# Mixture-of-experts stage: six steps of token rows in flight, the fifth group's weights in the last group's early place, later weights asked for over steps 3 to 12

## The reference

```
x = x + tanh(g_xattn[0]) * mamba(ctx_1024, layernorm(x))
x = x + tanh(g_ffn[0])   * moe(layernorm(x))
x = x + tanh(g_xattn[1]) * cross_attention(layernorm(x), ctx_1024, mask)
x = x + tanh(g_ffn[1])   * bitlinear_ffn(layernorm(x))

# moe: E = 64 experts, K = 8 choices a token, H = 256, I = 96, CAP = 64 places an expert
w, sel = top_k(softmax(x @ gate_w.T), K);  w = w / sum(w)
inp[e, slot] = x[tok]                        # the first 64 tokens that chose expert e
h   = silu(inp @ wg[e]) * (inp @ wu[e])      # (64 x 256) @ (256 x 96), twice
out = h @ wd[e]                              # (64 x 96) @ (96 x 256)
y[tok] += out[e, slot] * w
```

## Time and profile before

| what | value |
|---|---|
| median of 3 runs | 581.57 us (579.41 to 582.18) |
| profiled execution: own time | 579.86 us |
| profiled execution: span of the page | 577.9 us |
| mean granted TensorE clock | 0.953 of full |
| PE busy over the span | 478.6 us (83%) |
| DVE busy | 473.6 us (82%) |
| ACT, POOL busy | 365.2 us (63%), 280.9 us (49%) |
| DMA | 48.63 MB, mean 84 GB/s |

### The profile page before, as it was taken

How to read it: one execution, slowest core, us unless ns; L and a number is a source line. 1 busy time by engine, 2 the same in 40 slices (tenths; PEclk the granted TensorE clock), 3 DMA queues, 4 the chain that set the end, 5 groups by cost and what they waited for, 6 DMA issues and landing times.

```text
span 577.9 us, 10286 instructions
## 1 busy us (share of the span) xinstructions
PE 478.6 (83%) x3070; PEld 361.1 (62%) x3080; DVE 473.6 (82%) x1249; ACT 365.2 (63%) x831; POOL 280.9 (49%) x263
## 2 busy tenths in 40 slices
PE   5817777757769889999899999998789988998735
PEld 3302222122348856776788999997689878997714
DVE  4899999999995737888666856996899969875887
ACT  2785555535434645688776666679656796679543
POOL 4118777869420465550278368623875243323211
PEclk9956999999997989999999999999999999999877
DMA  5939400001052979894412012400335000000000
GB/s 155 233 76 325 120 0 1 1 1 36 1 157 80 308 217 294 212 313 144 180 52 73 2 29 65 56 1 2 47 55 66 0 2 2 19 2 0 1 19 20
DMA packets 45626, 48.63 MB, mean 84 GB/s; under 512 B 5660, under 2 KB 42118, under 8 KB 45574
## 3 DMA queue, kind: packets, MB, share of 16 engines
q1 hardware_dynamic: 41734, 36.46, 22.2%
q0 software_dynamic: 3840, 11.54, 9.3%
HBM read 41.43 MB, written 6.56 MB: 83 GB/s over the span
## 4 chain that ended last, share of the span: by engine, by line
PE 37%; DVE 21%; issue 20%; POOL 9%; ACT 7%; DMA 3%; SPq 1%; DVEq 1%; POOLq 0%; ACTq 0%; another core or an unknown queue 0%
DVE hst L1880 7%; PE ps L1619 6%; PE ps L1558 5%; PE ps L1559 5%; PE ps L1560 5%; PE ps L1608 3%; PE ps L1476 2%; DMA G<-token_rows,idx_x 2%; POOL dbu L586 2%; PE ps L1277 2%; POOL G L672 2%; POOL pn L688 2%; DVE hc L1889 2%; POOL G L650 1%; PE ps L1374 1%
## 5 line engine op out<-in xcount | busy, mean ns | idle before, releaser
L688 POOL TENSOR_TENSOR pn<-pr,pinv 128x512 f32<-128x512 f32 x64 | 67.7, 1060 | 87.3 <-DVE pinv L2289 86.9
L586 POOL TENSOR_TENSOR dbu<-du,brow 128x512 f32<-128x512 f32 x64 | 81.5, 1285 | 41.4 <-DVE du L1873 23.1
L1277 PE MATMUL ps<-hc,ident 128*128 128x512 f32 x128 | 72.7, 657 | 27.5 <-DVE hc L1889 26.0
L1880 DVE TENSOR_TENSOR_SCAN hst<-ps,dbu 128x512 f32<-128x512 f32 x64 | 77.6, 1213 | 0.2 <-POOL dbu L586 0.2
L831 ACT ACTIVATE ps<-dtv,amat 128x510 f32<-128x510 f32 x64 | 44.1, 690 | 49.1 <-DVE hst L1880 48.2
L1019 ACT ACTIVATE pr<-ebuf,smin 128x256 f32<-128x256 f32 x128 | 63.7, 501 | 13.7 <-DVE smin L2280 6.9
L1619 PE MATMUL ps<-pT,cS 128*128 128x256 f32 x256 | 66.5, 382 | 0.0
L1277 PEld LDWEIGHTS ps<-hc,ident 128*128 128x128 f32 x128 | 20.3, 195 | 66.8 <-DVE hc L1889 63.6
L650 POOL DMA_INDIRECT G<-token_rows,idx_x x32 | 38.1, 1192 | 48.3 <-DVE wkv L2015 24.0
L672 POOL DMA_INDIRECT G<-expert_out,idx_g x48 | 51.6, 1074 | 11.6 <-issue 10.2
L2280 DVE CUSTOM_DVE_ANT_0 ebuf<-ps,mbias 128x256 f32<-128x256 f32 x128 | 48.9, 419 | 4.1 <-issue 4.0
(11 more groups left out here) (380 smaller groups left out, 1377.3 us busy)
## 6 DMA issues: line engine op xcount, KB each, us to landing
wdn<-in_L_ffn_wd SPq DMA_DIRECT2D x12, 384.0 KB, 9.6
wgu<-in_L_ffn_wg SPq DMA_DIRECT2D x11, 384.0 KB, 7.0
wgu<-in_L_ffn_wu SPq DMA_DIRECT2D x11, 384.0 KB, 9.7
expert_out<-xn SPq DMA_DIRECT2D x11, 256.0 KB, 6.8
wq<-in_L_xattn_Wq SPq DMA_DIRECT2D x2, 1024.0 KB, 9.2
wo<-in_L_xattn_Wo SPq DMA_DIRECT2D x1, 2048.0 KB, 15.7
wo<-in_L_ffn_w SPq DMA_DIRECT2D x2, 1024.0 KB, 7.0
expert_out<-pexp SPq DMA_DIRECT2D x5, 256.0 KB, 3.3
```

The lines of the kernel that those rows point to most:

```text
L586: nc.gpsimd.tensor_tensor(dbu[:, j, :], du[:, j % 2, 512 * hb:512 * hb + 512], brow[:, j // 2, :], ALU.mult).then_inc(pool_dbu, 1)
L688: nc.gpsimd.tensor_tensor(pn[:, h % 2], pr[:, h % 2], pinv[:, h % 2, :].unsqueeze(2).to_broadcast([P, 2, L]), ALU.mult)\
L1277: pe.matmul(bank(2 + j % 2), ident[:], hc[:, j % 2, :], start=(isinstance(m, int) and m + k == 0), stop=(isinstance(m, int) and m + k == N ...
L1880: V.tensor_tensor_scan(hst[:, j, :], bank(j % 2), dbu[:, j, :], 0.0, ALU.mult, ALU.add)\
```

## The change

The row ring grows from four groups to six (`ROWS = 6`), which takes the place of group 4's gate and up weights in `G`. Two semaphores of a later stage serve the two new places, and that stage's waits are raised by 64 for it. POOL's gathers of groups 4 and 5 wait for `wqT_in_psum`, those from 6 on for `hg_ready` of group g-6. Group 4 takes the early places `wgu_last` and `wdn_last`; group 12 goes to the same places once group 4 is done, and groups 8 to 11 and 13 to 15 go to the ring. SP asks for gate and up of groups 8 to 15 in steps 3, 4, 5, 7, 8, 9, 10 and 11, for down one step later each. On TensorE `gate_up` of groups 1 and 2 is put ahead of `turn_rows` of groups 2 and 3.

```diff
+ROWS = 6
...
+        gate_up_homes = [*(wgu[:, k] for k in range(RING)), wgu_last[:], *(w[:] for w in early_gate_up)]
+        down_homes = [*(wdn[:, k] for k in range(RING)), wdn_last[:], *(w[:] for w in early_down)]
+
+        def home(g):
+
+            if g < 2 * RING:
+                return g
+            return (g - 2 * RING) % (RING + 1)
...
+        xe_flat = G[:].rearrange("p a k h -> p (a k h)")[:, 0:ROWS * 2 * ROW]
+        xe = xe_flat.rearrange("p (s q w) -> p s q w", s=ROWS, q=2)
...
             def gate_up_load(g):
-                slot = gate_up_slot(g)
-                if g == RING:
-                    sp_.wait_ge(wqT_in_psum, NKV)
-                elif RING + EARLY < g < NG - 1:
-                    sp_.wait_ge(gu_done, g - 7 if g < 12 else g - 3)
...
+                if g > RING + EARLY:
+                    sp_.wait_ge(gu_done, g - 7 if g <= 3 * RING else g - 4)
...
             def down_load(g):
-                if g == RING:
-                    sp_.wait_ge(down_done, 1)
-                elif RING + EARLY < g < NG - 1:
-                    sp_.wait_ge(down_done, g - 6 if g < 12 else g - 3)
...
+                if g > RING + EARLY:
+                    sp_.wait_ge(down_done, g - 7 if g <= 3 * RING else g - 4)
...
-            gate_up_load(NG - 1)
-            down_load(NG - 1)
+            gate_up_load(RING)
+            down_load(RING)
...
-            gate_up_load(RING)
             for s in range(NG + 2):
-                if s < 2:
-                    gate_up_load(s + 8)
-                if s == 2:
-                    down_load(RING)
-                    gate_up_load(10)
-                if s in (4, 9, 10, 11):
-                    gate_up_load(11 if s == 4 else s + 3)
-                if 2 < s < 7:
-                    down_load(s + 5)
-                if 9 < s < 13:
-                    down_load(s + 2)
+                for g in range(2 * RING, NG):
+                    if s == (6 * g - 36) // 5 + 1:
+                        gate_up_load(g)
+                    if s == (6 * g - 36) // 5 + 2:
+                        down_load(g)
                 if s > 1:
                     put(s - 2)
...
             def take_rows(g):
-                if g >= RING:
-                    pool.wait_ge(hg_ready, g - RING + 1)
+                if g >= ROWS:
+                    pool.wait_ge(hg_ready, g - ROWS + 1)
+                elif g >= RING:
+                    pool.wait_ge(wqT_in_psum, NKV)
...
             for g in range(NG + 3):
+                if g in (1, 2):
+                    gate_up(g)
                 if g + 1 < NG:
                     turn_rows(g + 1)
-                if 0 < g < NG:
+                if 2 < g < NG:
                     gate_up(g)
```

More of the change, by code:

```diff
@@ L230, in build_program, with gate_up_weights, down_weights @@
         prep_scope.close()
[L232 to L254, removed]
+        gate_up_homes = [*(wgu[:, k] for k in range(RING)), wgu_last[:], *(w[:] for w in early_gate_up)]
[4 more added lines that the diff above has]
+            return (g - 2 * RING) % (RING + 1)
+        def gate_up_weights(g):
+            return gate_up_homes[home(g)]
+        def down_weights(g):
+            return down_homes[home(g)]
         G = sb("G", [P, 2, K, H])
[L259 to L261 removed]
+        xe_flat = G[:].rearrange("p a k h -> p (a k h)")[:, 0:ROWS * 2 * ROW]
+        xe = xe_flat.rearrange("p (s q w) -> p s q w", s=ROWS, q=2)
         spare = sb("spare", [P, 2])
@@ L322, in gate_up_landed @@
                 return d_w[g], 48
-            if g == NG - 1:
+            if g == RING:
                 return d_ffn, 48
-            if g == RING:
-                return d_zero, 64
             if g <= RING + EARLY:
                 return early_landed[g - RING - 1]
-            return d_w[g % RING], 48 + 32 * (g // RING - 1)
+            if home(g) == RING:
+                return d_ffn, 48 + 32 + 32
+            return d_w[home(g)], 48 + 32 * (1 if g < 3 * RING else 2)
         def down_landed(g):
[L333 to L340, removed]
+            if g <= RING + EARLY:
+                return gate_up_landed(g)
+            if home(g) == RING:
+                return d_zero, 32 + 16
+            s, before = down_ring[home(g)]
+            return s, before + 16 * (1 if g < 3 * RING else 2)
         d_rows = sem("d_rows")
@@ L658, in _ @@
             pool.wait_ge(idx_x_ready, 1)
-            for g in range(RING):
-                take_rows(g)
-            for g in range(RING, NG):
+            for g in range(NG):
                 take_rows(g)
@@ L1498, in down @@
                                          hT[:, g % 2, P * q + CAP * e:P * q + CAP * e + CAP],
-                                         down_weights(slot)[0:I, 2 * q + e, :], start=True, stop=True)
+                                         down_weights(g)[0:I, 2 * q + e, :], start=True, stop=True)
                 last.then_inc(down_done, 1)
@@ L2210, in add_choices @@
                     if k < 2:
-                        dve.wait_ge(d_gath[cc][half], 8 * K * b)
+                        dve.wait_ge(d_gath[cc][half], 8 * K * b + (0 if cc else 64))
                 if k > 1:
```

25 lines of the change are left out of this document (11 added, 14 removed).

## The result

The changed kernel took 584.6 us (median of 20 runs, 579.45 to 590.14), the kernel before 579.53 us in the runs beside it. The ratio is 1.007, with a 95% interval of 1.0047 to 1.0092: slower by 0.7%, where 577.8 us and 3.8 us faster had been forecast, which beside these runs would be 575.7 us. The execution profiled here is one of those four, 589.66 us, with a span of 587.6 us and a clock of 0.93; its sizes are therefore too large, but the same places return in e10, an execution at the median.

A forecast was written before the change was run, and what follows sets the result against it. The stage was taken as a TensorE pipeline with two holes from late token rows, DMA the possible second bound. Gains 2.35 + 1.3 + 0.1, taken as 3.8 us, gave 581.57 - 3.8 = 577.8 us; range 575.0 to 582.3.

The forecast's parts named there:

- The start: First steps of the stage: product of group 1 fills TensorE's 2.30 us idle before turn 2; 2.35 us gained.
- half clock behind the hole: TensorE at 208 to 210 us: clock 0.50 after the idle before turn 2; expected to go with that idle.
- The second hole: Turn of group 6 waits 1.17 us for rows; asked for earlier, step 4 goes from 5.78 to 4.44 us: 1.3 gained.
- The sum: Whole stage: 2.35 + 1.3 + 0.1 = 3.75, taken as 3.8 us gained.
- The bytes: DMA from 212.8 to 265.1 us: 14.5 MB must land, at 294 GB/s with the last landing; costed at nothing.
- it fits, without much to spare: Verdict on DMA from 212.8 to 265.1 us: 294 GB/s asked, against 292 and 314 moved in full stretches.
- rival B: DMA bound in earnest, steps 9 to 15: +3.5 us, 585.1; slower than before under 273 GB/s average; chance 0.10.
- rivals A and B: DMA engines become the bound: A a little, 580.3 us, chance 0.18; B in earnest, 585.1 us, chance 0.10.
- 1.3 us beat: POOL's gathers, free of waits up to group 6, continue every 1.3 us (1.00 plus 0.30) behind 207.82.
- step 3: TensorE's step from turn 4 to turn 5: forecast to begin at 211.4 to 211.7 us, before at 213.92.

The follow-up runs named there:

- e10: The changed kernel, unaltered, run a third time in another set beside the kernel before: 585.64 us, ratio 1.0107.
- e5: The changed kernel, unaltered, in new rounds beside the kernel before: 577.75 us against 578.76, ratio 0.9978.
- e2: The changed kernel with TensorE's old order of gate and up products and turns: 578.57 us, ratio 0.9991.
- e13: The changed kernel, unaltered, run again as the measure for e14 and e15: 578.22 us against 580.43 before, ratio 0.994.
- e11: The changed kernel with gate and up of groups 8 to 15 asked for one step earlier: 585.27 us, ratio 1.0108.
- e14: The changed kernel with gathers four groups behind the gated product and gate and up of groups 8 to 15 one step earlier: 576.23 us, ratio 0.9956.
- e15: The kernel of e11 with pauses in POOL's row of gathers before groups 3, 4, 5, 7 and 8: 577.43 us, ratio 0.9953.
- e12: The changed kernel with gate and up of groups 13 to 15 loaded for 4 of 128 partitions only: 585.0 us, ratio 1.01.
- e9: The kernel before, unaltered, measured against itself: 581.15 us against 578.82, ratio 1.0025.
- e16: The kernel of e14 once more, in a set with late releases: 581.95 us against 581.58 before, ratio 1.0014.
- e17: The kernel of e15 once more, without late releases: 577.98 us, ratio 0.9987.
- e18: The changed kernel with TensorE's old order, gathers unbroken, and the old list of steps for the weights: 578.44 us, ratio 0.9994.

## Why the prediction was wrong

**The start** (2.35 us) was right where nothing is released late: from turn 0 to turn 4 e5 takes 212.80 - 202.00 = 10.80 us, before 13.50, so 2.7 us. The half clock behind the hole went with the hole. The new order, which the working leaned on, was the small part: with the old one e2 takes 212.94 - 201.73 = 11.21 us, so most of it came from rows and weights that no longer meet. **The second hole** (1.3 us) was right: 4.45 us a step. **The sum** of 3.8 us is 4.13 us at turn 15 in e5, the same up to turn 12 in e13.

**The bytes**: "it fits, without much to spare" failed as a cost of nothing. 1.24 us came back in e5, 1.47 in e2, 1.7 in e10, all of it in e13's one execution. The average rate was not short: in 212 to 230, 230 to 248 and 248 to 262 e5 moved 273, 328 and 281 GB/s, a mean of 295 where 294 had been asked, and e13 271, 317 and 259, a mean of 284, above rival B's 273. I had left out that gate and up of 12 to 15 stand in four steps in a row, and that SyncE's issues lengthen in such a stretch, so that the stores stand behind them. e11, e14 and e15 ask earlier, e12 for less, and each has a tail of 15.4 us. The waits are those that rivals A and B named, in `take_out` on a store and in e13 in the product on weights; the average rate, which they named as the cause, gives by their working nothing for e5 and 1.8 us of the 4.4 for e13.

**The step that failed** is the one that I did not write: that 16 gathers in an unbroken row cost the others nothing. "POOL is free of waits up to group 6, so it continues its 1.3 us beat" was right as a beat. But in the four profiles of changed kernels in two sets turn 3 is released 4.3 us late, 1.5 to 1.6 us after that beat ends: 20.6 to 23.9 us to turn 5 instead of 15.4. In the terms of the sum, for the first profile: from turn 0 to turn 4 it took 12.88 us, 0.6 gained and not 2.35, and step 3, from turn 4 to turn 5, had no term at all and took 10.99 us where it had taken 4.55. In e10, whose clock stayed full there, these are 12.89 and 7.72 us. e10's stage is 3.4 us longer than that of before in the same set (e9), 1.7 up to turn 5 and 1.7 of tail. The medians of that set lie 6.8 us apart; no profile shows the other half. That it is the row, and neither TensorE's order nor an idle SyncE queue, is argued and not shown: for it are turn 2, which keeps time with POOL's gathers, and one pair, e11 and e16, which differ in nothing else but come from two sets: 20.59 and 16.85 us. e17 and e18, meant to confirm it, met no late release. The row is not enough by itself, since e5, e13 and e18 have it unbroken and release in time, and the kernel before has a late release too, in e9. What sets this way of running apart, and through what the row holds a release up, stays open. Every execution here was recorded, so no run shows whether the late release is there without the recording. That the same traces lack records is a hint: the Trainium skill (NOTIFIC — the notification-queue block, "Overflow: three behaviours, one of which stalls the engine") says that the block which writes such records holds its sources back inside rather than lose one, and that it counts such stalls, where a count above zero would mean that an engine had been slowed. By that alone no record would be missing, so the missing ones want something more. No run here shows that this is what happened. In the other sets the change is 0.998 [0.9951, 1.0004] and 0.994 [0.9906, 0.9973].

**The size of the gain in the time.** Even there 4.1 us of pipeline made 1.0 us of median in e5 and 2.2 in e13. The tail took 1.2 or more, and the one profile I took all absolute times from was 0.2 to 1.1 us ahead of all others at the matmul that starts at 24.25 us. What is left of the difference no profile explains.

**A version that does better.** e14 has a lower median than the changed kernel beside it (576.2 against 578.2 us), but their ratios, 0.9956 and 0.994, do not tell them apart; its stage is 3.7 us shorter than in the one profile of e13 and 0.6 us shorter than in e5. In a set with late releases (e16) it is even with before, where the changed kernel was 0.7 and 1.1% slower in two other such sets. e15 has the shorter stage. Both were faster than before in their set (0.9956 [0.9925, 0.9986], 0.9953 [0.9923, 0.9983]).

## What to carry to other kernels

An average rate that fits is not enough: spread transfers over the stretch, and count a queue's issue times among its load, since a store behind loads pays for all of them. When a wait is taken from an engine, ask what unbroken run it makes, and who lives off its pauses. Before explaining a small loss, run the same kernel again in another set: here the same code was 0.994 and 1.011.

## What the runs showed of the hardware

Beside POOL's unbroken row of gathers a finished turn was taken up by ScalarE 4.3 us late, 1.5 us after the row, and the one before it 0.2 to 0.8 us late during the row, in some sets of rounds and not in others; one chip gave one profile of either kind. SyncE's issue of a store took 0.37 us in the kernel before, also with a DMA share of 1.06 around it, and up to 3.38 us in e13 in a stretch of 18 us at 1.08. The first 24 us, whose code is the same in all these kernels, differ by 1.1 us from one execution to another. A fall of the clock at 174 us, ahead of the stage, is worth 3.1 us: from the matmul next to it to turn 0 it is 27.40 us in e13, with 0.50 in 174 to 178, and 24.30 in e14, with 1.00.
